# Crossed quadrants for two of four pairs in an inversion by halves, in a twelve-stage decoder kernel on one core

## The chip, the core and the metric

The kernel runs on one core of one Trainium2 chip. Its time is the device time of one execution in microseconds (us). The whole network, four layers of three stages each, runs in one launch; the four batch elements are four passes of a loop. The change touches the first stage of a pass only.

## The reference, cut to what matters

The first layer's attention is a gated delta rule over 512 tokens with 16 heads of 64 values, two heads of v for each head of q and k:

```python
def step(S, xs):
    q_t, k_t, v_t, g_t, b_t = xs
    S = S * jnp.exp(g_t)[..., None, None]
    kv = jnp.einsum('bhk,bhkv->bhv', k_t, S)
    S = S + jnp.einsum('bhk,bhv->bhkv', k_t, (v_t - kv) * b_t[..., None])
    o_t = jnp.einsum('bhk,bhkv->bhv', q_t, S)
    return (S, o_t)
S0 = jnp.zeros((b_, HV, DK, DV), jnp.float32)
_, oT = jax.lax.scan(step, S0, (qT, kT, vT, gT, bT))
```

Taken 128 tokens at a time this scan needs, for each head, the inverse of a unit lower triangular matrix of 128x128 that is made of k times k, the decays and b. The outputs, the state for the next 128 tokens, and all later stages follow from it.

## The kernel before, in words

The function `stage_l0_attn` computes the inverse by halves. The 128 rows are two blocks of 64, TOP (partitions 0 to 63) and LOW (64 to 127). In each block an inverse X of blocks of 1, 2, 4, ... rows is doubled level by level, L = 6 levels in all; levels 1 to 5 double inside the blocks, level 6 makes the corner between TOP and LOW. X and its transpose XT are both kept, in `xx` (index 0 and 1). A level l < 6 is: `half_level`, AX = part times X (L2622), where `part` is the level's share of the matrix, masked by GpSimd (L2810); a copy of AX from PSUM to `ax` by ScalarE (L2744); `whole_level`, the products X AX (L2637) and AX XT (L2641); and VectorE's subtraction of both from `xx` (L2912, at level 5 L2916 and L2919, which write `solved`). Level 6 is L2618, L2744 on 64 rows, L2632, and ScalarE's `corner` (L2752).

The heads are taken two at a time (a pair), four pairs in one step (p = 0 to 3), eight steps in a pass (n = 0 to 7; 128 tokens of half of the heads each). FIRST is the pairs 0 and 1, SECOND the pairs 2 and 3. PSUM bank p belongs to pair p of the inversion: columns 0 to 127 for AX, 128 to 255 for the change of X, 256 to 383 for that of XT. Every matmul on a block has 64 rows and 64 columns of TensorE, and for levels 1 to 5 it reads and writes the same block, TOP to TOP or LOW to LOW: two of the array's four quadrants. A f32 matmul is two MATMUL records in the trace.

Between the levels of step n every engine does, in an order written out by hand, the work around the inversion: of the coming step `prep` (L2532, L2536; decays by ScalarE L2694 and L2699; VectorE L2837 to L2843) and `turn` (L2544: the transpose of `part0`; VectorE L2854 and L2856 make the first XT and X from it), and of the past step `ks` (L2565, VectorE L2868), `corrected` (L2582, ScalarE L2724 and L2734), `output` (L2591, VectorE L2883 or a copy) and `add` (L2601, VectorE L2898). TensorE's order in a step:

- level 1: half, ks FIRST of the past, whole, prep FIRST of the coming
- level 2: half, corrected FIRST, whole
- level 3: half, output FIRST, whole, turn FIRST
- level 4: half, add FIRST, prep SECOND, whole, ks SECOND
- level 5: half, corrected SECOND, whole, output SECOND, turn SECOND
- level 6: half, whole, add SECOND

VectorE's order: ks FIRST, whole 1; whole 2, prep FIRST; output FIRST, whole 3, turn FIRST; add FIRST, whole 4, ks SECOND, prep SECOND; whole 5, turn SECOND; output SECOND, add SECOND. Step 0 has no past work, steps 1 and 2 no ks (their state products are still zero), step 7 no coming work.

Each engine goes through its queue in order, and waits on counting semaphores: `x_less` (VectorE's update of a pair is done), `ax_psum`, `ax_ready`, `xx_psum`, `part_ready`, `x0_ready` (the first X of a pair), `a_turned` (turn is done).

Of the kernel before, what the change touches and what calls it, by code (L numbers as in the profile page):

```python
# [21 lines left out]
ALU = mybir.AluOpType  # L22
# [3 lines left out]
P = 128  # L26
# [2182 lines left out]
def stage_l0_attn(m):  # L2209
# [16 lines left out]
    with ExitStack() as ctx:  # L2226
# [248 lines left out]
        a_turned = sem("a_turned")  # L2475
        x0_ready = sem("x0")
# [46 lines left out]
        with nc.Block(no_gpsimd_drain=True) as block:  # L2523
            @block.tensor
            def _(pe):
# [13 lines left out]
                def turn(n, pairs):  # L2539
                    for p in pairs:  # L2540
# [5 lines left out]
                        ins.then_inc(a_turned, 1)  # L2546

# [57 lines left out]
                def half_level(n, l):  # L2605

                    for p in range(4):
                        if l == 1:
                            pe.wait_ge(x0_ready, unit(n, p) + 1)
                            if n >= 1:  # L2610
                                pe.wait_ge(corner_ready, unit(n - 1, p) + 1)
                        else:
                            pe.wait_ge(x_less, at_less(n, l - 1, p))
                        if l < L:
                            pe.wait_ge(part_ready, at_less(n, l, p))
                        for i in range(2):
                            if l == L:
                                ins = pe.matmul(m.psum[LOW, p, W * i:W * i + W], ab[TOP, n % 2, p, i, W:P],  # L2618
                                                xx[TOP, n % 2, p, X, i, :], start=True, stop=True)
                            else:  # L2620
                                for b in BLOCKS:
                                    ins = pe.matmul(m.psum[b, p, W * i:W * i + W], part[b, (M * n + l - 1) % 2, p, i, :],  # L2622
                                                    xx[b, n % 2, p, X, i, :], start=True, stop=True)
                        ins.then_inc(ax_psum, 1)

                def whole_level(n, l):

                    for p in range(4):
                        pe.wait_ge(ax_ready, at(n, l, p))
                        if l == L:  # L2630
                            for i in range(2):
                                ins = pe.matmul(m.psum[TOP, p, 256 + W * i:256 + W * i + W], ax[LOW, p, i, :],  # L2632
                                                solved[LOW, n % 2, p, i, W:P], start=True, stop=True)
                        else:
                            for i in range(2):
                                for b in BLOCKS:
                                    pe.matmul(m.psum[b, p, P + W * i:P + W * i + W], xx[b, n % 2, p, XT, i, :],  # L2637
                                              ax[b, p, i, :], start=True, stop=True)
                            for i in range(2):
                                for b in BLOCKS:  # L2640
                                    ins = pe.matmul(m.psum[b, p, 256 + W * i:256 + W * i + W], ax[b, p, i, :],  # L2641
                                                    xx[b, n % 2, p, XT, i, :], start=True, stop=True)
                        ins.then_inc(xx_psum, 1)
# [9 lines left out]
                for pairs in (FIRST, SECOND):  # L2653
                    prep(0, pairs)
                    turn(0, pairs)
                for n in range(STEPS + 1):
# [769 lines left out]
```

## Time and profile before

| | |
|---|---|
| median of 3 runs | 4809.8 us (4809.14 to 4811.06) |
| profiled execution | 4809.4 us |
| its span, first to last instruction | 4807.6 us |
| granted TensorE clock, mean | 0.922 |
| TensorE matmul / weight load busy | 4044.5 us (84%) / 2481.0 us (52%) |
| VectorE / ScalarE / GpSimd busy | 2463.6 (51%) / 1545.1 (32%) / 820.3 us (17%) |

The profiled execution is 1.8 us longer than its span. A busy share of TensorE is of modelled ends: matmuls are pipelined, each record of a 64x64 f32 matmul lasts 0.22 us, and many are in flight at a time, so that starts say more than durations. In pass 1 the eight steps of the inversion begin at 120.6 us; in pass 2 they begin at 1322.7 us.

### The profile page before, as it was taken

Reading aid. Unit: us, or ns where it says so; the run is one execution under the profiler, and the core shown is the slowest. Engines: PE = TensorE matmul, PEld = TensorE weight load, DVE = VectorE, ACT = ScalarE, POOL = GpSimd, SP = SyncE. Lnnn points to the kernel's source line nnn. Section 1 sums busy time; section 2 is a strip of 40 time slices with the busy share of each in tenths; the row PEclk is TensorE's granted clock in tenths of the full one; section 3 lists DMA queues with packets and bytes.
Section 4 is the critical chain, followed back from the end, with each engine's and each line's share of the span. In section 5 each row is a group of like instructions: output and inputs, shape, how many; then the busy total and the mean of one; then the engine's idle time right before and its main releaser. Section 6 shows DMA issues by size and latency. Waiting matters only on the chain. (4 is left out here: it accounts for less than half of the span.)

```text
span 4807.6 us, 96693 instructions
## 1 busy us (share of the span) xinstructions
PE 4044.5 (84%) x38412; PEld 2481.0 (52%) x38412; DVE 2463.6 (51%) x6030; ACT 1545.1 (32%) x3476; POOL 820.3 (17%) x1436
## 2 busy tenths in 40 slices
PE   6997787898799778789879977878987998787888
PEld 3884343465388334346548833434654873343464
DVE  5664444454566443445456645345545664533554
ACT  3442222341344222234134422223413442222341
POOL 1430000130143000013014300001201430001120
PEclk8999999999799999999979999999997999999999
DMA  2000000000000000000000010000000001000000
GB/s 79 3 3 16 41 18 17 22 35 25 25 3 3 16 41 18 17 22 35 25 25 3 3 39 18 18 17 22 35 25 25 3 3 56 1 18 17 22 35 27
DMA packets 11006, 105.56 MB, mean 22 GB/s; under 512 B 1149, under 2 KB 5553, under 8 KB 6193
## 3 DMA queue, kind: packets, MB, share of 16 engines
q1 hardware_dynamic: 10544, 99.21, 5.4%
q8 instruction: 314, 5.14, 0.4%
q14 instruction: 148, 1.20, 0.1%
HBM read 98.16 MB, written 1.05 MB: 21 GB/s over the span
## 5 line engine op out<-in xcount | busy, mean ns | idle before, releaser
L88 PE MATMUL psum<-ident_bf 128*128 128x512 bf16 x1928 | 540.6, 420 | 201.5 <-DVE l_attn_peak L770 66.5
L88 PEld LDWEIGHTS psum<-ident_bf 128*128 128x128 bf16 x1928 | 190.7, 106 | 480.1 <-issue 170.6
L2912 DVE TENSOR_TENSOR l_attn_xx<-l_attn_xx,psum 128x256 f32<-128x256 f32 x512 | 206.1, 419 | 209.6 <-PE psum L2641 197.4
L2744 ACT ACTIVATE l_attn_ax<-psum 128x128 f32<-128x128 f32 (+1 forms) x768 | 184.7, 279 | 357.0 <-PE psum L2622 242.3
L399 DVE TENSOR_TENSOR l_ffn_hidden<-l_ffn_silu,psum 128x512 f32<-128x512 f32 (+2 forms) x184 | 126.4, 687 | 325.2 <-ACT l_ffn_silu L340 325.1
L94 PEld LDWEIGHTS psum<-streamed_weights,l_ffn_hidden 128*128 128x128 f32 (+2 forms) x1728 | 226.0, 192 | 113.4 <-issue 100.2
L340 ACT ACTIVATE l_ffn_silu<-psum 128x512 f32<-128x512 f32 (+2 forms) x216 | 128.9, 597 | 475.9 <-PE psum L310 475.9
L2637 PE MATMUL psum<-l_attn_ax,l_attn_xx 64*64 64x64 f32 x5120 | 266.0, 222 | 0.0
L2641 PE MATMUL psum<-l_attn_xx,l_attn_ax 64*64 64x64 f32 x5120 | 259.2, 220 | 0.0
L770 DVE TENSOR_REDUCE l_attn_peak<-psum 128x4 f32<-128x2048 f32 (+3 forms) x128 | 185.8, 1487 | 122.7 <-PE psum L688 121.7
L2810 POOL TENSOR_TENSOR l_attn_part<-l_attn_ab,streamed_weights 128x128 f32<-128x128 f32 x640 | 242.6, 414 | 27.4 <-PE psum L2622 27.4
L94 PE MATMUL psum<-streamed_weights,l_ffn_hidden 128*128 128x128 f32 (+2 forms) x1728 | 229.9, 276 | 9.1 <-DVE l_ffn_hidden L396 5.0
L787 DVE RECIPROCAL l_attn_inverse<-psum 128x512 f32<-128x512 f32 x20 | 67.2, 3358 | 292.5 <-PE psum L722 292.5
L2637 PEld LDWEIGHTS psum<-l_attn_ax,l_attn_xx 64*64 64x64 f32 x5120 | 205.9, 136 | 17.3 <-issue 9.3
L746 ACT ACTIVATE l_attn_prob<-psum 128x2048 f32<-128x2048 f32 (+1 forms) x96 | 152.9, 1593 | 184.7 <-PE psum L707 184.7
L2641 PEld LDWEIGHTS psum<-l_attn_xx,l_attn_ax 64*64 64x64 f32 x5120 | 206.2, 137 | 0.0
L2622 PE MATMUL psum<-l_attn_xx,l_attn_part 64*64 64x64 f32 x5120 | 197.7, 224 | 8.4 <-POOL l_attn_part L2810 6.0
L2622 PEld LDWEIGHTS psum<-l_attn_xx,l_attn_part 64*64 64x64 f32 x5120 | 177.6, 137 | 28.1 <-issue 13.4
L164 ACT ACTIVATE xnT<-psum 128x256 f32<-128x256 f32 x80 | 29.9, 384 | 463.1 <-PE psum L177 459.2
L309 PE MATMUL psum<-l_ffn_gated_x,streamed_weights 128*128 128x512 f32 (+1 forms) x320 | 169.4, 611 | 4.5 <-DVE l_ffn_gated_x L378 4.5
L760 POOL TENSOR_SCALAR_AFFINE_SELECT l_attn_prob<-l_attn_prob 128x512 f32<-128x512 f32 x128 | 80.0, 637 | 540.6 <-ACT l_attn_prob L746 540.6
L2431 DVE SCALAR_TENSOR_TENSOR l_attn_conv<-psum,streamed_weights,l_attn_conv 128x511 f32<-128x511 f32 (+2 forms) x192 | 142.3, 748 | 54.8 <-ACT l_attn_conv L2361 50.3
(514 smaller groups left out, 8131.1 us busy)
## 6 DMA issues: line engine op xcount, KB each, us to landing
streamed_weights<-pack_l_ffn SPq DMA_DIRECT2D x4, 5412.0 KB, 16.5
streamed_weights<-pack_l_ffn SPq DMA_DIRECT2D x4, 3972.0 KB, 12.6
streamed_weights<-pack_l_attn SPq DMA_DIRECT2D x5, 2848.5 KB, 9.5
streamed_weights<-pack_l_xattn SPq DMA_DIRECT2D x4, 2496.0 KB, 8.6
streamed_weights<-pack_l_ffn SPq DMA_DIRECT2D x4, 2192.0 KB, 8.3
streamed_weights<-pack_l_xattn SPq DMA_DIRECT2D x4, 2048.0 KB, 8.5
streamed_weights<-pack_l_ffn SPq DMA_DIRECT2D x4, 1923.0 KB, 8.1
streamed_weights<-pack_l_attn SPq DMA_DIRECT2D x4, 1107.5 KB, 5.2
```

The lines of the kernel that those rows point to most:

```text
L88: pe.matmul(self.bank(bank), self.ident_bf[:, :], self.ident_bf[:, :].unsqueeze(1).to_broadcast([P, NT, P]), start=True, stop=True)
L94: ins = pe.matmul(self.psum[:, OUT, t * P:(t + 1) * P], features[:, t * P:(t + 1) * P], weight, start=first and t == 0, stop=last, skip_gr ...
L309: pe.matmul(m.bank(n % 2)[0:r], w["up"][:, c:c + r], rhs, start=True, stop=True)
L746: act.activation(prob[:, u % SLOTS, :, 0:used(part)], m.psum[:, 0:R, 0:used(part)], ACT.Exp).then_inc(exps_ready, 1)
L770: dve.tensor_reduce(peak[:, g, i, :], m.psum[:, base:base + R, 0:(i + 1) * P], AX, ALU.max, negate=True).then_inc(peak_ready, 1)
L2431: ins = dve.scalar_tensor_tensor(out=later, in0=m.psum[:, n % 2, 0:T - 3 + i], scalar=w["conv_w"][:, ORDER[n], i:i + 1], in1=later, op0=AL ...
L2622: ins = pe.matmul(m.psum[b, p, W * i:W * i + W], part[b, (M * n + l - 1) % 2, p, i, :], xx[b, n % 2, p, X, i, :], start=True, stop=True)
L2637: pe.matmul(m.psum[b, p, P + W * i:P + W * i + W], xx[b, n % 2, p, XT, i, :], ax[b, p, i, :], start=True, stop=True)
L2641: ins = pe.matmul(m.psum[b, p, 256 + W * i:256 + W * i + W], ax[b, p, i, :], xx[b, n % 2, p, XT, i, :], start=True, stop=True)
L2744: act.activation(ax[b, p, :, :], m.psum[b, p, 0:P].rearrange("p (i t) -> p i t", i=2), ACT.Copy).then_inc(ax_ready, 1)
L2810: pool.tensor_tensor(part[:, q % 2, p, :, :], ab[:, n % 2, p, :, 0:W], over_block(w["levels"][:, l, :]), ALU.mult).then_inc(part_ready, 1)
L2912: dve.tensor_tensor(both, both, m.psum[:, p, P:384], ALU.subtract).then_inc(x_less, 1)
```

## The change

For the odd pairs (p = 1 and 3, "crossed") the half level's product reads block b and writes the other block, and the X product of the whole level comes back the same way. So the plain pair uses the quadrants TOP to TOP and LOW to LOW, and the crossed pair TOP to LOW and LOW to TOP. In `xx` the crossed pair has X and XT in swapped places (`kind`), with XT on the other block than X. ScalarE gives `ax` a scale of -1 for crossed pairs, and VectorE adds where it subtracted. The XT product of a crossed pair, for levels 1 to 4, reads and writes one block, into columns 384 to 511 of the plain neighbour's bank; at level 5 it goes across, on top of an identity product that carries the old XT across.

The products of two pairs are now issued interleaved, after the waits of both. VectorE's update of a plain pair waits for its neighbour's products too. To bring the first XT of a crossed pair onto the other block there is a new step `move` of TensorE (one identity product per head and block, into the place in PSUM that `turn` filled, hence after VectorE has taken X from there, `x0_taken`), and of VectorE (the subtraction from the identity). TensorE has it after half level 4 (FIRST) and half level 6 (SECOND), VectorE at the start of its levels 4 and 6.

```diff
+        def crossed(p):
+            return p % 2 == 1
+        def side(p, b):
+            return {0: LOW, W: TOP}[b.start] if crossed(p) else b
+        def kind(p, which):
+            return 1 - which if crossed(p) else which
...
+                def move(n, pairs):
+                    for p in pairs:
+                        if crossed(p):
+                            pe.wait_ge(a_turned, unit(n, p) + 1)
+                            pe.wait_ge(x0_taken, unit(n, p) // 2 + 1)
+                            for i in range(2):
+                                for b in BLOCKS:
+                                    ins = pe.matmul(m.psum[side(p, b), 4 + p % 2, W * i:W * i + W],
+                                                    w["ident_blocks"][b, :], part0[b, p % 2, i, :], start=True, stop=True)
+                            ins.then_inc(moved, 1)
...
                 def half_level(n, l):
-                    for p in range(4):
...
+                    def product(p, i, b):
+                        return pe.matmul(m.psum[side(p, b), p, W * i:W * i + W], part[b, (M * n + l - 1) % 2, p, i, :],
+                                         xx[b, n % 2, p, kind(p, X), i, :], start=True, stop=True)
+
+                    for pairs in (FIRST, SECOND):
...
                         if l < L:
+                            for i in range(2):
+                                for p in pairs:
+                                    for b in BLOCKS:
+                                        ins = product(p, i, b)
+                                    if i == 1:
+                                        ins.then_inc(ax_psum, 1)
...
                 def whole_level(n, l):
+                    def x_product(p, i, b):
+                        s = side(p, b)
+                        pe.matmul(m.psum[b, p, P + W * i:P + W * i + W], xx[s, n % 2, p, kind(p, XT), i, :], ax[s, p, i, :],
+                                  start=True, stop=True)
+
+                    def xt_product(p, i, b):
+                        s = side(p, b)
+                        old = xx[s, n % 2, p, kind(p, XT), i, :]
+                        if crossed(p) and l == M:
+                            out = m.psum[b, p, 256 + W * i:256 + W * i + W]
+                            pe.matmul(out, w["ident_blocks"][s, :], old, start=True, stop=False)
+                            return pe.matmul(out, ax[s, p, i, :], old, start=False, stop=True)
+                        out = m.psum[s, p - 1, 384 + W * i:384 + W * i + W] if crossed(p) else \
+                            m.psum[s, p, 256 + W * i:256 + W * i + W]
+                        return pe.matmul(out, ax[s, p, i, :], old, start=True, stop=True)
+
+                    for pairs in (FIRST, SECOND):
+                        for p in pairs:
+                            pe.wait_ge(ax_ready, at(n, l, p))
...
                         if n < STEPS:
                             half_level(n, l)
+                        if l == 4:
+                            coming(n, move, FIRST)
+                        elif l == 6:
+                            coming(n, move, SECOND)
...
+                        act.activation(ax[b, p, :, :], m.psum[b, p, 0:P].rearrange("p (i t) -> p i t", i=2), ACT.Copy,
+                                       scale=-1.0 if crossed(p) and l < L else 1.0).then_inc(ax_ready, 1)
...
-                        dve.tensor_tensor(xx[:, n % 2, p, XT, :, :], one, part0[:, p % 2, :, :], ALU.subtract)
+                        if not crossed(p):
+                            dve.tensor_tensor(xx[:, n % 2, p, XT, :, :], one, part0[:, p % 2, :, :], ALU.subtract)
...
+                def move(n, pairs):
+                    one = w["ident_blocks"].unsqueeze(1).to_broadcast([P, 2, W])
+                    for p in pairs:
+                        if crossed(p):
+                            dve.wait_ge(moved, unit(n, p) // 2 + 1)
+                            dve.tensor_tensor(xx[:, n % 2, p, kind(p, XT), :, :], one, heads(m.psum[:, 4 + p % 2, 0:P]),
+                                              ALU.subtract).then_inc(x0_ready, 1)
...
-                        dve.wait_ge(xx_psum, at(n, l, p))
+                        dve.wait_ge(xx_psum, at(n, l, p if crossed(p) else p + 1))
```

## Rows read from the trace of the kernel before

**Rows 1.** The page: engines busy; costliest groups (busy, mean ns, idle before, releaser).

```profile
PE 4044.5 (84%) x38412; PEld 2481.0 (52%) x38412; DVE 2463.6 (51%) x6030; ACT 1545.1 (32%) x3476; POOL 820.3 (17%) x1436
...
L2637 PE MATMUL psum<-l_attn_ax,l_attn_xx 64*64 64x64 f32 x5120 | 266.0, 222 | 0.0
```

**Rows 2.** Windows, whole steps: us, then busy us of each engine, granted clock, DMA.

```profile
147.45:176.62 29.17, 28.73 (x607) 25.96 (x605) 18.27 (x59) 14.05 (x55) 12.81 (x28) 0.92 0.01 3
1349.03:1376.23 27.20, 26.76 (x602) 23.91 (x600) 18.36 (x59) 13.82 (x55) 12.80 (x28) 1.00 0.01 3
233.08:262.06 28.98, 28.28 (x617) 25.07 (x617) 20.98 (x73) 14.85 (x60) 12.82 (x28) 1.00 0.01 3
1322.65:1349.03 26.38, 24.05 (x561) 21.39 (x561) 16.82 (x52) 10.49 (x39) 15.25 (x35) 0.93 0.01 3
```

**Rows 3.** Order of time, TensorE in a steady step: start, us, engine, line, count.

```profile
236.81 1.13 PE L2532 MATMUL psum<-l_attn_gu,w_const 128*128 128x256 f32 x4
237.88 0.70 PE L2536 MATMUL psum<-l_attn_qk 64*128 64x256 f32 x4
...
240.90 0.40 PE L2641 MATMUL psum<-l_attn_xx,l_attn_ax 64*64 64x64 f32 x8
...
242.30 0.40 PE L2641 MATMUL psum<-l_attn_xx,l_attn_ax 64*64 64x64 f32 x8
...
248.44 0.44 PE L2601 MATMUL psum<-l_attn_u_end,l_attn_k 128*64 128x128 f32 x4
...
250.50 0.45 PE L2637 MATMUL psum<-l_attn_ax,l_attn_xx 64*64 64x64 f32 x8
```

**Rows 4.** Order of time, VectorE in the same step, levels 2 and 3.

```profile
241.35 1.82 DVE L2912 TENSOR_TENSOR l_attn_xx<-l_attn_xx,psum 128x256 f32<-128x256 f32 x4 [4.00 <-PE psum L2641]
243.09 0.41 DVE L2837 TENSOR_TENSOR l_attn_ab<-l_attn_decay,psum 64x256 f32<-64x256 f32 x1
...
246.39 1.41 DVE L2912 TENSOR_TENSOR l_attn_xx<-l_attn_xx,psum 128x256 f32<-128x256 f32 x4
```

**Rows 5.** Order of time, TensorE where level 6's half meets turn.

```profile
258.79 0.27 PE L2618 MATMUL psum<-l_attn_xx,l_attn_ab 64*64 64x64 f32 x1
258.83 0.28 PE L2544 MATMUL psum<-streamed_weights,l_attn_part 64*64 64x64 f32 x3
258.89 0.22 PE L2618 MATMUL psum<-l_attn_xx,l_attn_ab 64*64 64x64 f32 x1
258.90 0.27 PE L2544 MATMUL psum<-streamed_weights,l_attn_part 64*64 64x64 f32 x2
...
259.01 0.70 PE L2618 MATMUL psum<-l_attn_xx,l_attn_ab 64*64 64x64 f32 x9
```

**Rows 6.** Order of time, all engines, the steady step's end.

```profile
256.81 0.28 DVE L2916 TENSOR_TENSOR l_attn_xx<-l_attn_xx,psum 128x128 f32<-128x128 f32 x1
...
260.06 0.42 DVE L2854 TENSOR_TENSOR l_attn_xx<-streamed_weights,l_attn_part 128x128 f32<-128x128 f32 x1
260.08 0.27 PE L2618 MATMUL psum<-l_attn_xx,l_attn_ab 64*64 64x64 f32 x1 [0.37 <-DVE l_attn_solved L2919]
...
260.32 1.01 PE L2632 MATMUL psum<-l_attn_solved,l_attn_ax 64*64 64x64 f32 x13
...
260.86 0.78 ACT L2752 ACTIVATE l_attn_solved<-psum 64x128 f32<-64x128 f32 x4
...
261.53 0.60 PE L2601 MATMUL psum<-l_attn_u_end,l_attn_k 128*64 128x128 f32 x4 [0.20 <-DVE l_attn_v L2883]
```

**Rows 7.** Windows, columns as in rows 2: pass 1, pass 2, a steady step's end.

```profile
145.20:151.90 6.70, 6.53 (x108) 6.34 (x110) 2.72 (x9) 2.51 (x10) 1.12 (x4) 0.50 0.00 0
...
142.50:145.00 2.50, 1.53 (x24) 0.98 (x18) 2.36 (x11) 0.36 (x2) 2.37 (x6) 1.00 0.03 7
1345.00:1348.00 3.00, 1.64 (x23) 1.09 (x20) 2.82 (x12) 0.82 (x3) 3.00 (x9) 1.00 0.02 5
257.50:260.90 3.40, 3.03 (x55) 2.80 (x53) 3.22 (x13) 1.06 (x5) 2.84 (x8) 1.00 0.00 0
```

More of the change, by code:

```diff
@@ L2475, in stage_l0_attn @@
         a_turned = sem("a_turned")
+        x0_taken = sem("x0_taken")
+        moved = sem("moved")
         x0_ready = sem("x0")
@@ L2605, in half_level @@
                 def half_level(n, l):
-                    for p in range(4):
[L2608 to L2613, printed above, removed]
-                        if l < L:
-                            pe.wait_ge(part_ready, at_less(n, l, p))
-                        for i in range(2):
-                            if l == L:
[L2618 to L2630, printed above, removed]
-                            for i in range(2):
[L2632 to L2643, printed above, removed]
+                    def product(p, i, b):
+                        return pe.matmul(m.psum[side(p, b), p, W * i:W * i + W], part[b, (M * n + l - 1) % 2, p, i, :],
+                                         xx[b, n % 2, p, kind(p, X), i, :], start=True, stop=True)
@@ new lines, in whole_level @@
+                def whole_level(n, l):
+                    def x_product(p, i, b):
[15 more added lines that the diff above has]
+                            pe.wait_ge(ax_ready, at(n, l, p))
+                            if l == L:
+                                for i in range(2):
+                                    ins = pe.matmul(m.psum[TOP, p, 256 + W * i:256 + W * i + W], ax[LOW, p, i, :],
+                                                    solved[LOW, n % 2, p, i, W:P], start=True, stop=True)
+                                ins.then_inc(xx_psum, 1)
+                        if l < L:
+                            for i in range(2):
+                                for p in pairs:
+                                    for b in BLOCKS:
+                                        x_product(p, i, b)
+                            for p in pairs:
+                                for i in range(2):
+                                    for b in BLOCKS:
+                                        ins = xt_product(p, i, b)
+                                ins.then_inc(xx_psum, 1)
@@ L2655, in _ @@
                     turn(0, pairs)
+                    move(0, pairs)
                 for n in range(STEPS + 1):
@@ L2910, in whole_level @@
                         if l < M:
-                            both = xx[:, n % 2, p, :, :, :].rearrange("p a i t -> p (a i t)")
-                            dve.tensor_tensor(both, both, m.psum[:, p, P:384], ALU.subtract).then_inc(x_less, 1)
+                            both = xx[:, n % 2, p, :, :, :].rearrange("p a i t -> p a (i t)")
+                            if crossed(p):
+                                change = m.psum[:, p - 1:p + 1, :].rearrange("p n c -> p (n c)")[:, 384:896].rearrange(
+                                    "p (a c) -> p a c", a=2)[:, :, 0:P]
+                                ins = dve.tensor_tensor(both, both, change, ALU.add)
+                            else:
+                                change = m.psum[:, p, P:384].rearrange("p (a c) -> p a c", a=2)
+                                ins = dve.tensor_tensor(both, both, change, ALU.subtract)
+                            ins.then_inc(x_less, 1)
                         else:
@@ L2925, in _ @@
                     turn(0, pairs)
+                    move(0, pairs)
                 for n in range(STEPS + 1):
@@ L2933, in _ @@
                             output(n - 1, FIRST)
+                        if more and l == 4:
+                            move(n + 1, FIRST)
+                        if more and l == 6:
+                            move(n + 1, SECOND)
                         if last and l == 4:
```

33 lines of the change are left out of this document (25 added, 8 removed).

## The prediction

> **What bounds the kernel now.** I read the page first, for the engines' shares and the lines of the first layer's inversion [rows 1]; then the stage's steps one by one, which say what a step costs and at which clock [rows 2]; then the order of time inside one steady step, TensorE and VectorE side by side, since only that shows which wait ends last [rows 3 to 6]; and last the granted clock around the one place where it fell inside the stage [rows 7].
>
> The stage is four passes (one per batch element) of eight steps. A steady step takes 28.98 us, of which TensorE is busy 28.28 and VectorE 20.98 at a granted clock of 1.00 [rows 2]. So the naive reading is that TensorE bounds it, and that fewer TensorE microseconds are worth their full price. The order of time says less. Level 3's x updates run on VectorE back to back, four in 1.41 us (0.33 us from start to start), behind a preparation that began at 243.09; level 2's four came at TensorE's pace, 1.82 us [rows 4]. At the end of the step TensorE waits outright: L2618 of the last pair starts at 260.08, right after VectorE's L2919, and L2601 at 261.53 after L2883 [rows 6]. VectorE has 20.7 us of starts per step and each group of them hangs on a TensorE result. I count time inside the steady step from 233.08 = 0.
>
> **Beats.** A 64x64 f32 matmul is two records. Groups of eight records on the two diagonal quadrants follow each other every 0.23 us (240.90 to 242.30 is six of them [rows 3]), so two records, one per quadrant, start each 58 ns: I call this a beat. Do other quadrants run beside them? The trace of before has the case: L2618 goes from the upper rows to the lower columns. Its records start at 258.79, 258.89 and 259.01 with one between the last two, and among them L2544, on the diagonal, keeps starting at 258.83 and 258.90 [rows 5]. So three quadrants run at a beat each, although two of them share their rows and two their columns. I take four records per beat for the changed kernel.
>
> The Trainium skill, "TensorE: Matmul & The Clock Gate", Part 3 (What overlaps and what doesn't), says that a weight load overlaps a running matmul only where their row groups differ, which speaks against this change: a plain and a crossed pair share row groups. By the rule TensorE would save nothing; the row above is against it, and the last rival is what it would give.
>
> **Part by part, TensorE per step.**
> - Half levels 1 to 5: 16 beats each become 8 (two groups of 4): 40 beats less, 2.34 us.
> - Whole levels 1 to 4: per two pairs 8 + 8 beats become 4 beats of x products on four quadrants, then 8 of XT products, which stay on the diagonal in both pairs: 8 less per level, 32 in all, 1.87 us.
> - Whole level 5: the crossed pairs' XT products go across and have an identity product added. Plain quadrants carry 4+4 beats, crossed ones 4+8, so 12 per two pairs if they overlap (16, as now, if not): 0.47 us or nothing. It is hidden either way, since VectorE is the later one there.
> - Added: two moves a step, 4 beats each, 0.23 us and a first beat of 0.05.
>
> Sum: 28.28 - 4.7 + 0.6, about 24.2 us of TensorE in a step. VectorE keeps the same number of instructions: a crossed pair's L2854 goes, the move's subtraction comes; L2919's subtraction becomes a copy. ACT's scale of -1 costs nothing: L2752 copies with it, four in 0.78 us [rows 6], as fast as any plain copy of ACT.
>
> **What waits are added.** Each pair of pairs is now waited for together, in half_level, whole_level and in VectorE's plain pair. The move is a round trip: VectorE's x0 of the crossed pair, TensorE's move, VectorE again. Behind TensorE's wait for it at level 4 stand add and prep of SECOND and whole level 4; at level 6 whole level 6 and add of SECOND. Latencies: from a last record's start to its reader 0.27 us (the group that starts at 242.30 and lasts 0.40 has its last start at 242.48 [rows 3], and the fourth update starts 0.42 before the end of its row, at 242.75 [rows 4]); from an instruction's end to a waiting TensorE 0.05 (VectorE's level 5 ends at 260.03, L2618 starts at 260.08 [rows 6]).
>
> **The steady step, chained by hand.** Level 1: half 0 to 0.5, ks to 1.3, whole to 2.75, prep (L2532 and L2536, 236.81 to 238.51, 1.7 us [rows 3]) to 4.6; before 5.43. Level 2: half to 5.1, corrected to 6.25, whole to 7.65. VectorE's prep starts when level 2's updates are through, at 8.65 for 10.0 before: 1.36 us are gained here. Level 3: VectorE runs without a gap, prep 2.78, output 0.53, four updates 1.33 [rows 4], and the crossed x0 ends 0.75 later (by the turn of SECOND, which starts at 260.06 [rows 6]), at 14.03. TensorE's move waits for it, so add starts at 14.4 for 15.36, and whole level 4 at 16.5 for 17.42 [rows 3]: of 1.36 us 0.9 are left. Whole level 4 is 0.47 shorter, so VectorE's prep of SECOND starts at 19.6 for 20.96: 1.36 again. From there VectorE is the bound: prep 2.78, four times 0.81 for level 5 (256.81 to 260.06 [rows 6]), ending at 25.65. The x0 of SECOND is done at 26.55; TensorE's move runs 26.6 to 26.85; whole level 6 (L2632, 16 records on one quadrant, one per beat, as x13 in 1.01 us) ends its starts at 27.8; add and the switch of shapes 0.7 as at 261.53 to 262.06, next step at 28.5. Before whole level 6 started at 27.02 beside the last L2618; now it starts at 26.9 for all of VectorE's lead. So a steady step gains 0.5 us of the 4.1 that TensorE saves.
>
> **The others.** Steps 1 and 2 have no state products: 27.20 us at full clock [rows 2]. The same chain gains 0.9 at level 2's end, 0.5 at add, 0.6 at VectorE's second prep, and the end gives 0.85 back: 0.2 us slower. Step 0: level 1 is cold (clock 0.93 over the step), the shorter products gain 0.9, given back at the end: 0. Step 7 has no next step to prepare, so no moves: 1.0 faster (bounds 0.5 and 1.3). Before step 0 the move lies open once: 0.9 slower. Steps 3 to 6: 4 x 0.5. Per pass 2.0 - 0.4 + 0 + 1.0 - 0.9 = 1.7 us faster, four passes 6.8. Each hand-made step may be off by 0.5 us either way, one way in all: 32 x 0.5 = 16 us.
>
> **The clock.** That sum holds at 2.4 GHz. In pass 1 the clock fell to 1.2 GHz (0.50) at the end of step 0 and stayed there for the 6.70 us of the row [rows 7]. What TensorE did before: short bursts of L2618 between waits for VectorE, busy 1.53 of 2.50 us. In pass 2 the same place was busy 1.64 of 3.00 and the clock held; so too in passes 3 and 4. In the steady step the place is dense, 3.03 of 3.40, and it never fell. The price: step 1 took 29.17 us in pass 1 and 27.20 in pass 2 [rows 2], 1.97 us. After the change every step's end looks like step 0's: TensorE has done output and turn at 24.1 and until 26.9 it has three bursts of L2618 and the move, about 1.6 us of record time in 3.0. It then faces level 1 and 2, where TensorE is the path and VectorE idle, so a low clock is paid in full. There are 7 such ends in a pass, 28 in all. One in four fell in the rows; by the single-quadrant stretch that follows (move, then whole level 6) I take two in five: 11, which is 10 more than before, 19.7 us. Ends: none (clock holds) and half of them plus the tails, 18, 34 us.
>
> Sum against the profiled execution, 4809.4 us (span 4807.6, 1.8 around it; the median is 4809.8): 4809.4 - 6.8 + 19.7 = 4822.3 us.
>
> **Rivals.**
> - The clock holds. For it: three of four sparse ends of step 0 held. Against: 28 chances. 4809.4 - 6.8 = 4802.6 us.
> - TensorE is the bound as its share says. For it: 28.28 of 28.98. All of it reaching the end gives 4.1 x 32 = 131 us, 4678; VectorE's gapless stretch [rows 4] is against. Its milder form, 1.0 us a step more than my chain, because waits overlap better than I drew, gives 4802.6 - 28 = 4775, or with five falls 4785.
> - Quadrants that share rows take turns. TensorE then saves nothing, the moves lie open: 0.4 us at level 4 and 0.9 at the step's end, 28 x 1.3 = 36 us: 4846 us. [rows 5] is against it; the skill's rule of Part 3 named above would give this.
>
> **How the numbers follow.** A measurement of this kernel can tell 0.2%, 9.6 us, from no change, so the bounds are 4800.2 and 4819.4. The forecast, falls of the clock at the steps' ends: 0.47, of it 0.42 above the bound and 0.05 (few falls) inside. Clock holds: 0.28, of it 0.05 below. More gained than my chain has: 0.20, all faster. Turns: 0.05, slower. So faster 0.25, same 0.28, slower 0.47. The likeliest case alone spans 4811 (seven falls, less gain) to 4843 (18 falls, chain gain near 0). The range must take in the clock-holds case with some of its error, down to 4795, and leaves the rest of the third case and the last outside: 4795 to 4843.
>
> **What would show it.** Right: L2622's 32 records in about half their time when both groups are ready; steady steps of about 28.5 us where the clock is 1.00; gaps in TensorE at the end of levels 2, 3 and 5, released by VectorE; TensorE's move waiting for the crossed x0 with whole level 6 behind it; granted clock 0.50 at some steps' starts, two in five, mean clock about 0.915 for 0.922. Wrong: a clock of 1.00 through all steady steps (then 4803), steady steps under 28 us (the hand chain has a wait too many), or L2637's crossed records 58 ns behind the plain ones (turns).

## The result, and the profile after

The changed kernel takes 4878.3 us (median of 4 runs, 4872.6 to 4884.9) beside 4810.4 us for the kernel before on the same chip (4 runs): ratio 1.014, 95% interval 1.0122 to 1.0157. The forecast was 4822.3 us with a range to 4843. The sign was right, the size was not. The profiled execution took 4881.4 us (span 4879.7), which is 72.0 us more than that of before; I forecast 12.9 more. TensorE's busy time hardly moved, by the first lines of the page (busy us and share of the span):

```profile
PE 4037.4 (83%) x39436; PEld 2431.4 (50%) x39436; DVE 2445.9 (50%) x6030; ACT 1535.0 (31%) x3476; POOL 817.0 (17%) x1436
...
L2633 PE MATMUL psum<-l_attn_xx,l_attn_part 64*64 64x64 f32 x5120 | 151.2, 244 | 56.0 <-DVE l_attn_xx L2982 33.0
L2663 PE MATMUL psum<-l_attn_ax,l_attn_xx 64*64 64x64 f32 x5120 | 172.8, 241 | 2.3 <-ACT l_attn_ax L2800 2.3
```

L2663 was L2637, with 266.0 us [rows 1]; the half level's product is now L2633. The second line's end is the new thing: TensorE waits 56.0 us ahead of the half levels, most of it for VectorE's update of a crossed pair (L2982).

Windows of whole steps after, columns as in [rows 2]: step 0, two second steps (pass 1 and 2), a third step, two steady steps, and all of pass 1's inversion:

```profile
121.40:150.56 29.16, 23.95 (x593) 19.75 (x593) 16.32 (x52) 10.04 (x39) 14.79 (x34) 0.85 0.01 3
150.56:180.10 29.54, 26.52 (x635) 22.59 (x633) 17.70 (x58) 13.64 (x54) 12.74 (x28) 0.90 0.01 3
1363.70:1393.20 29.50, 26.49 (x636) 22.59 (x635) 17.64 (x58) 13.67 (x54) 12.74 (x28) 0.90 0.01 3
180.12:209.77 29.65, 26.57 (x634) 22.54 (x632) 18.27 (x60) 13.07 (x52) 12.74 (x28) 0.90 0.01 3
239.78:270.93 31.15, 28.22 (x648) 23.98 (x648) 20.57 (x72) 14.68 (x60) 12.73 (x28) 0.89 0.02 4
270.93:300.66 29.73, 26.84 (x650) 22.72 (x648) 20.58 (x72) 14.57 (x60) 12.73 (x28) 0.95 0.01 3
121.40:348.24 226.84, 201.84 (x4894) 171.23 (x4896) 143.03 (x485) 100.47 (x407) 94.64 (x212) 0.91 0.01 3
```

Before, a steady step took 28.98 us at 1.00 and a second step 27.20 [rows 2]. Now none of these windows has a clock of 1.00. The last column but two is to be read first: 0.85 to 0.95. Windows around the ends of steps, as in [rows 7], and one of the few ends at which the clock held:

```profile
178.50:185.30 6.80, 6.60 (x114) 5.70 (x113) 2.49 (x9) 1.91 (x8) 0.00 (x0) 0.50 0.01 2
239.90:243.30 3.40, 3.40 (x76) 3.06 (x77) 1.68 (x8) 1.62 (x8) 0.00 (x0) 0.50 0.02 7
267.20:274.00 6.80, 6.28 (x94) 5.33 (x94) 3.00 (x14) 2.54 (x12) 0.00 (x0) 0.50 0.01 2
297.00:300.40 3.40, 2.30 (x34) 1.99 (x36) 2.43 (x10) 1.52 (x7) 1.19 (x4) 1.00 0.00 0
```

In pass 1 TensorE went down to 1.2 GHz at the ends of six of the seven steps that have a next one; all passes together, at 24 of 28, and twice more in the middle of step 0 (passes 2 and 4), where before it was 1 of 28. Summed over the four inversions the trace has 171.9 us of low clock, for 21.4 before (some 15 of these are left over from the stretch ahead of the inversions); the inversions themselves take 911.8 us, for 855.2 (from the start of a pass's first half-level record to the start of its last one, at level 5 of step 7). So 56.6 of the 72.0 us lie inside them.

What the end of a steady step looks like, TensorE, at full clock (start, us, engine, line; in brackets the idle time before and who ended it), and VectorE beside it. This is the end of step 5, at which the clock held:

```profile
297.14 0.44 PE L2648 MATMUL psum<-l_attn_xx,l_attn_ab 64*64 64x64 f32 x4 [0.18 <-DVE l_attn_solved L2996]
297.96 0.44 PE L2648 MATMUL psum<-l_attn_xx,l_attn_ab 64*64 64x64 f32 x4 [0.38 <-DVE l_attn_solved L2994]
298.98 0.45 PE L2569 MATMUL psum<-l_attn_part,streamed_weights 64*64 64x64 f32 x8 [0.58 <-DVE l_attn_xx L2915]
299.27 1.09 PE L2682 MATMUL psum<-l_attn_solved,l_attn_ax 64*64 64x64 f32 x16
300.30 0.44 PE L2626 MATMUL psum<-l_attn_u_end,l_attn_k 128*64 128x128 f32 x4
300.66 0.86 PE L2633 MATMUL psum<-l_attn_xx,l_attn_part 64*64 64x64 f32 x32
```

```profile
297.94 0.40 DVE L2913 TENSOR_TENSOR l_attn_xx<-streamed_weights,l_attn_part 128x128 f32<-128x128 f32 x1
298.35 0.48 DVE L2915 TENSOR_TENSOR l_attn_xx<-streamed_weights,psum 128x128 f32<-128x128 f32 x2
299.47 0.29 DVE L2923 TENSOR_TENSOR l_attn_xx<-streamed_weights,psum 128x128 f32<-128x128 f32 x1 [0.63 <-PE psum L2569]
```

The move (L2569) cannot start until VectorE has made the last x0 (L2915), and level 6's whole (L2682, L2632 of before) stands behind it. Before, L2632 had its first record at 260.10 beside the last L2618, 0.04 us after VectorE came to its last turn at 260.06 [rows 6]; now it starts 1.33 us after VectorE's last turn (297.94 to 299.27):

```profile
260.10 0.27 PE L2632 MATMUL psum<-l_attn_solved,l_attn_ax 64*64 64x64 f32 x1
```

The end of step 3 looked the same, and there the clock fell at 239.9; the end of step 6, where it fell at 328.6, too:

```profile
236.14 0.44 PE L2648 MATMUL psum<-l_attn_xx,l_attn_ab 64*64 64x64 f32 x4 [0.18 <-DVE l_attn_solved L2996]
236.96 0.44 PE L2648 MATMUL psum<-l_attn_xx,l_attn_ab 64*64 64x64 f32 x4 [0.38 <-DVE l_attn_solved L2994]
237.98 0.45 PE L2569 MATMUL psum<-l_attn_part,streamed_weights 64*64 64x64 f32 x8 [0.58 <-DVE l_attn_xx L2915]
...
326.95 0.44 PE L2648 MATMUL psum<-l_attn_xx,l_attn_ab 64*64 64x64 f32 x4 [0.38 <-DVE l_attn_solved L2994]
```

So the same idle times stand at ends that fell and at one that held. What decides between them no run here shows.

### The profile page after: what moved, and what is told of

Its sections match the earlier page's. It is cut to its first block and busy times, and to the rows that moved or that the text cites. A ratio compares the mean times of both kernels' runs of the same rounds, so it can differ in the third digit from the quotient of the medians.

```text
span 4879.7 us, 99197 instructions
## 1 busy us (share of the span) xinstructions
PE 4037.4 (83%) x39436; PEld 2431.4 (50%) x39436; DVE 2445.9 (50%) x6030; ACT 1535.0 (31%) x3476; POOL 817.0 (17%) x1436
## 5 line engine op out<-in xcount | busy, mean ns | idle before, releaser
L2800 ACT ACTIVATE l_attn_ax<-psum 128x128 f32<-128x128 f32 (+1 forms) x768 | 167.8, 278 | 386.4 <-PE psum L2633 281.8
L2985 DVE TENSOR_TENSOR l_attn_xx<-l_attn_xx,psum 128x256 f32<-128x256 f32 x256 | 107.3, 419 | 227.0 <-PE psum L2675 226.8
L2675 PE MATMUL psum<-l_attn_xx,l_attn_ax 64*64 64x64 f32 x4608 | 207.0, 231 | 0.1
L2633 PE MATMUL psum<-l_attn_xx,l_attn_part 64*64 64x64 f32 x5120 | 151.2, 244 | 56.0 <-DVE l_attn_xx L2982 33.0
L2675 PEld LDWEIGHTS psum<-l_attn_xx,l_attn_ax 64*64 64x64 f32 x4608 | 180.0, 147 | 0.4 <-issue 0.4
L2663 PE MATMUL psum<-l_attn_ax,l_attn_xx 64*64 64x64 f32 x5120 | 172.8, 241 | 2.3 <-ACT l_attn_ax L2800 2.3
L309 PE MATMUL psum<-l_ffn_gated_x,streamed_weights 128*128 128x512 f32 (+1 forms) x320 | 169.4, 611 | 4.5 <-DVE l_ffn_gated_x L378 4.5
L2633 PEld LDWEIGHTS psum<-l_attn_xx,l_attn_part 64*64 64x64 f32 x5120 | 117.7, 148 | 96.4 <-DVE l_attn_xx L2982 67.4
L310 PE MATMUL psum<-l_ffn_gated_x,streamed_weights 128*128 128x512 f32 (+1 forms) x320 | 163.4, 592 | 0.0
```

The lines of the kernel that those rows point to most:

```text
L309: pe.matmul(m.bank(n % 2)[0:r], w["up"][:, c:c + r], rhs, start=True, stop=True)
L310: pe.matmul(m.bank(2 + n % 2)[0:r], w["gate"][:, c:c + r], rhs, start=True, stop=True).then_inc(up_ready, 1)
L2633: return pe.matmul(m.psum[side(p, b), p, W * i:W * i + W], part[b, (M * n + l - 1) % 2, p, i, :], xx[b, n % 2, p, kind(p, X), i, :], start ...
L2663: pe.matmul(m.psum[b, p, P + W * i:P + W * i + W], xx[s, n % 2, p, kind(p, XT), i, :], ax[s, p, i, :], start=True, stop=True)
L2675: return pe.matmul(out, ax[s, p, i, :], old, start=True, stop=True)
L2800: act.activation(ax[b, p, :, :], m.psum[b, p, 0:P].rearrange("p (i t) -> p i t", i=2), ACT.Copy, scale=-1.0 if crossed(p) and l < L else 1 ...
```

## The experiments

The theories. A: what costs is the clock, which falls because TensorE's work at a step's end has become sparse. B: what costs is the added waits themselves, the pairs waited for together and the round trip of the move, at full clock. The further question was which piece of the change makes the end sparse.

Each was timed against the kernel before on the same chip; between the chips the kernel before differs by up to 3 us, so the ratios compare the kernels best. Low clock and inversion time in the table are sums over the four inversions of the profiled execution.

| kernel | us | ratio to before | steady step, us | inversions, us | low clock in them, us |
|---|---|---|---|---|---|
| before | 4810 | 1 | 28.98 | 855.2 | 21.4 |
| changed | 4878.3 | 1.014 (1.0122 to 1.0157) | 29.5 to 31.9 | 911.8 | 171.9 |
| e1: changed, filled ends | 4830.3 | 1.005 (1.0033 to 1.0068) | 29.06 | 872.3 | 37.7 |
| e2: before, filled ends | 4826.8 | 1.0037 (1.0025 to 1.005) | 29.46 | 864.3 | 13.8 |
| e3: pairs only, no crossing | 4852.5 | 1.0082 (1.0064 to 1.0101) | 29.72 | 896.6 | 26.4 |
| e4: both moves late | 4807.9 | 0.9991 (0.9979 to 1.0003) | 27.94 | 841.2 | 52.2 |
| e5: before with one wait | 4863.6 | 1.0109 (1.0093 to 1.0124) | 30.7 to 32.1 | 917.4 | 124.1 |
| e6: second move late | 4813.8 | 0.9996 (0.9985 to 1.0007) | 27.97 | 847.2 | 64.2 |
| e7: both late, step 0 filled | 4794.8 | 0.9967 (0.9955 to 0.9978) | 27.90 | 831.9 | 21.1 |
| e8: before, step 0 filled | 4805.4 | 0.9991 (0.9982 to 1.0001) | 29.01 | 853.3 | 14.0 |

**e1, the changed kernel with its ends filled.** Products that nobody reads stand ahead of TensorE's waits at the step's end.

```diff
+                def fill(count, bank):
+                    for _ in range(count):
+                        pe.matmul(m.psum[TOP, bank, 384:512], m.ident_bf[:, 0:W], m.ident_bf[:, :], start=True, stop=True)
...
+                                if l == L and p >= 1:
+                                    fill(4, p - 1)
                                 pe.wait_ge(x_less, at_less(n, l - 1, p))
...
                         elif l == 6:
+                            if n + 1 < STEPS:
+                                fill(4, 3)
                             coming(n, move, SECOND)
```

> The changed kernel with four small bf16 products (128 rows, 64 columns, 128 moving) before each wait for VectorE at level 6 and before the second move, where TensorE waits about 0.5 us each time. Theory A (the clock: it falls at the end of 24 of 28 steps, and that is the whole loss, since steps with little low clock take the 29.0 us of before): the clock stays at 1.00 through most steps, low time inside the stage falls from 165 us to under 60, steps of 29.0 to 29.3 us, 4815 to 4830 us. Theory B (the added waits are the loss and the clock is a bystander): the steps stay at 29.5 to 31.5 us plus the fill, 4878 or more.

**e2, the same fill in the kernel before**, ahead of level 6's waits, to price it.

```diff
+                            if l == L and p >= 1:
+                                fill(4, p - 1)
                             pe.wait_ge(x_less, at_less(n, l - 1, p))
```

> Control: the kernel before with the same products before the waits of level 6. Both theories: the stage was at full clock there already but for pass 1, so nothing to win beyond 2 us; the change of shapes costs at most 3 x 0.15 us a step where TensorE did not wait. 4808 to 4825 us.

A steady step and the whole inversion of pass 1, first of e1, then of e2:

```profile
234.52:263.58 29.06, 27.28 (x666) 22.95 (x664) 20.62 (x72) 14.69 (x61) 12.78 (x28) 1.00 0.02 4
121.80:338.05 216.25, 198.37 (x5005) 166.96 (x5008) 143.01 (x485) 100.25 (x407) 94.88 (x212) 0.99 0.01 4
```

```profile
232.05:261.51 29.46, 29.33 (x632) 25.85 (x630) 21.05 (x72) 14.92 (x60) 12.82 (x28) 1.00 0.01 3
120.60:336.70 216.10, 214.19 (x4756) 190.33 (x4756) 147.64 (x486) 103.73 (x408) 95.47 (x213) 0.99 0.01 3
```

More work on TensorE made the changed kernel 48 us faster. The low clock went from 171.9 to 37.7 us, and the step to 29.06 us at a clock of 1.00. The fill isn't free: three groups a step (the changed kernel has a fourth, ahead of the move) cost the kernel before 0.48 us a step (29.46 against 28.98) and 17 us in all, which is 2 us above the expected 4825. In the changed kernel a part of the fill stands in time in which TensorE would wait, so less than that is to be taken off; its own rows give 28.9 to 29.0 us for a steady step at full clock (see "The parts, added up"). Theory A's numbers hold, at their upper end, so most of the loss is the clock.

**e3, waits without crossing.** All pairs are plain and there are no moves; the order of the products and the waits for two pairs stay.

```diff
         def crossed(p):
-            return p % 2 == 1
+            return False
...
-                        dve.wait_ge(xx_psum, at(n, l, p if crossed(p) else p + 1))
+                        dve.wait_ge(xx_psum, at(n, l, p | 1))
```

> The changed kernel's loops and pair waits with no pair crossed, so no move and only the two diagonal quadrants. Theory A: TensorE has the beats of before (28.3 us in 29), is dense at the step's end, the clock holds, 4810 to 4825 us. Theory B, in the form that waiting for two pairs at a time costs: VectorE's first update is 0.47 us later at each of five levels, steps of 30 us or more at full clock, 4835 to 4880 us.

```profile
240.09:269.81 29.72, 28.51 (x619) 25.05 (x618) 20.74 (x73) 14.62 (x60) 12.80 (x28) 1.00 0.01 3
123.70:348.03 224.33, 212.81 (x4672) 187.65 (x4672) 144.21 (x486) 100.61 (x408) 95.21 (x212) 0.99 0.01 3
```

The waits in pairs have a price of their own, 0.74 us in a steady step and 2.3 in step 7 (18.48 us for 16.19, to its last half level), 41 us over the four inversions, but the clock stays up (26.4 us low): it falls at the end of step 0, in all four passes, and at no later end. So they don't bring the falls of the other steps. The time is what theory B expected, the clock what theory A did. This kernel also shows what crossing does to the products. A half level's 32 records at full clock, first here, then in the changed kernel:

```profile
245.50 1.15 PE L2633 MATMUL psum<-l_attn_xx,l_attn_part 64*64 64x64 f32 x32
```

```profile
276.82 0.70 PE L2633 MATMUL psum<-l_attn_xx,l_attn_part 64*64 64x64 f32 x32
```

Each row is 0.22 us longer than its starts: 0.93 and 0.48 us for 16 and 8 beats.

**e4, both moves late.** TensorE's move FIRST goes behind add FIRST, its move SECOND behind the whole of level 6; VectorE's move SECOND goes behind output SECOND.

```diff
-                        if l == 4:
-                            coming(n, move, FIRST)
-                        elif l == 6:
-                            coming(n, move, SECOND)
...
                             past(n, add, FIRST)
+                            coming(n, move, FIRST)
                             coming(n, prep, SECOND)
...
+                            coming(n, move, SECOND)
                             past(n, add, SECOND)
...
-                        if more and l == 6:
-                            move(n + 1, SECOND)
...
                             output(n - 1, SECOND)
+                        if more and l == 6:
+                            move(n + 1, SECOND)
```

> The changed kernel with the second move behind whole level 6 instead of ahead of it (VectorE's part behind its output), and the first behind add. The hand chain says whole level 6 starts 0.8 us earlier and the step is 0.7 to 0.9 us shorter in 28 steps, clock falls unchanged: 4853 to 4860 us. Rival: the next step's half level 1 then waits for the x0 of the last pair and gets all of it back: 4870 to 4880 us. If the denser end also keeps the clock up in some steps: under 4850 us.

The end of a steady step, and windows of such a step and of the inversion:

```profile
283.72 0.44 PE L2648 MATMUL psum<-l_attn_xx,l_attn_ab 64*64 64x64 f32 x4 [0.18 <-DVE l_attn_solved L2994]
284.54 0.27 PE L2648 MATMUL psum<-l_attn_xx,l_attn_ab 64*64 64x64 f32 x1 [0.38 <-DVE l_attn_solved L2992]
...
284.78 1.01 PE L2682 MATMUL psum<-l_attn_solved,l_attn_ax 64*64 64x64 f32 x13
285.57 0.45 PE L2569 MATMUL psum<-l_attn_part,streamed_weights 64*64 64x64 f32 x8
285.95 0.44 PE L2626 MATMUL psum<-l_attn_u_end,l_attn_k 128*64 128x128 f32 x4
286.32 0.88 PE L2633 MATMUL psum<-l_attn_xx,l_attn_part 64*64 64x64 f32 x32
```

```profile
230.34:258.28 27.94, 25.71 (x651) 21.58 (x648) 20.50 (x73) 14.42 (x60) 12.74 (x28) 1.00 0.01 4
121.10:330.38 209.28, 188.47 (x4893) 158.88 (x4896) 142.31 (x485) 98.72 (x407) 94.65 (x212) 0.98 0.01 4
```

The gaps of 0.18 and 0.38 us are still there; the one of 0.58 is gone. From the start of the last L2648 group to the next step it is now 1.78 us (284.54 to 286.32), for 2.70 in the changed kernel (297.96 to 300.66), both at full clock. The time is below the figures that both theories gave by the chain; what came true is the clause on a denser end. The same products, the moves among them put elsewhere, take 70 us less, and the clock no longer falls in any steady step. What low clock is left lies in step 0, where it also falls in the middle in two passes, and in the first 4 us of step 1.

**e5, the kernel before with that one wait.** TensorE waits for the last x0 ahead of level 6's whole; nothing else is changed.

```diff
+                        if l == L and n + 1 < STEPS:
+                            pe.wait_ge(x0_ready, unit(n + 1, 3) + 1)
                         if n < STEPS:
                             whole_level(n, l)
```

> The kernel before with one wait more: TensorE's whole level 6 waits until VectorE has made the last pair's x0 of the coming step, as the move of SECOND makes it wait in the changed kernel. No crossing, no move. The wait holds whole level 6 back by VectorE's last turn, about 0.75 us (L2854 of SECOND starts at 260.06 in the steady step, the first record of L2632 at 260.32, a crossed x0 ends at about 260.8 to 261). Theory A (a wait for VectorE at the step's end costs itself, and the sparse end then lets TensorE's clock fall): steady steps 29.5 to 29.9 us at full clock, the clock falls at many of the 28 step ends, low clock in the stage 60 us or more against 21, in all 4840 to 4870. Theory B (the wait costs only itself; the falls come from the shorter products of the crossed kernel): steady steps 29.5 to 29.9, low clock in the stage 20 to 35 us, in all 4825 to 4838. If the wait is hidden by the last L2618 (a third way): steps 29.0 to 29.2, 4810 to 4816.

```profile
262.94 0.44 PE L2618 MATMUL psum<-l_attn_xx,l_attn_ab 64*64 64x64 f32 x4 [0.37 <-DVE l_attn_solved L2921]
264.09 1.14 PE L2632 MATMUL psum<-l_attn_solved,l_attn_ax 64*64 64x64 f32 x16 [0.71 <-DVE l_attn_xx L2858]
265.17 0.44 PE L2601 MATMUL psum<-l_attn_u_end,l_attn_k 128*64 128x128 f32 x4
265.53 1.27 PE L2622 MATMUL psum<-l_attn_xx,l_attn_part 64*64 64x64 f32 x19
```

```profile
265.60:269.00 3.40, 3.40 (x49) 3.06 (x50) 1.31 (x6) 1.11 (x4) 0.00 (x0) 0.50 0.02 5
234.17:265.59 31.42, 30.21 (x620) 26.79 (x619) 21.16 (x72) 15.23 (x60) 12.78 (x28) 0.93 0.01 3
118.10:346.94 228.84, 219.46 (x4672) 195.88 (x4672) 147.78 (x486) 105.45 (x408) 95.39 (x213) 0.93 0.01 3
```

One idle time of 0.71 us, in the kernel before, brings 51 us and 124 us of low clock; the clock falls at 21 of 28 ends. Crossed quadrants are not needed for the loss. Theory A's numbers hold (124.1 us low for "60 or more", 4863.6 for "4840 to 4870"). The wait holds whole level 6 back by more than the 0.75 us named there, since in the kernel before its first record stands at 260.10 and not at 260.32.

**e6, only the second move late**: e4's edit without its move of FIRST, which stays ahead of add FIRST.

> The changed kernel with only the second move (SECOND, at the step's end) taken away from its place: TensorE's half of it behind the whole of level 6, VectorE's behind output SECOND. The first move stays ahead of add FIRST. With both moves late the kernel took 4807.85 us, steady steps 27.9 us at full clock, low clock in the stage 52 us. Theory A (the whole excess of the changed kernel comes from the second move): steady steps 27.9 to 28.1, low clock 40 to 65 us, 4806 to 4814. Theory B (the first move's round trip at level 4 holds add and whole level 4 back by 0.5 us or more): steady steps 28.4 or more, 4820 to 4830.

```profile
235.00:262.97 27.97, 25.65 (x654) 21.65 (x652) 20.60 (x72) 14.43 (x60) 12.76 (x28) 1.00 0.01 4
```

27.97 against 27.94: the first move costs next to nothing where it stood. The second is the whole excess over this kernel. Theory A's numbers hold.

**e7, a candidate for the best version.** e4 and, in step 0 alone, products that nobody reads.

```diff
+                        if n == 0 and l == 4 and pairs == FIRST:
+                            fill(8)
                         for p in pairs:
+                            if n == 0 and l == L and p >= 1:
+                                fill(5)
```

> Both moves late, and in step 0 of each pass bf16 products of 128x128 that nobody reads: eight before level 4's half of FIRST, five before each wait of level 6. What low clock is left with both moves late lies at the end of step 0 and in step 1 (1284.6 to 1346.1 and 148.0 to 151.4, 52 us over four passes, about 0.35 us of time per us of it). Theory A (these falls come from the sparse end of step 0): the low clock in the stage falls to 25 us or less, 4796 to 4804. Theory B (they come from what stands before the stage or from phase, and the added products cost their own time): low clock 40 us or more, 4808 to 4816.

Step 0, a steady step, and pass 1's inversion:

```profile
124.50:151.86 27.36, 24.07 (x615) 19.65 (x616) 16.03 (x51) 10.11 (x40) 14.81 (x34) 0.89 0.01 3
232.92:260.82 27.90, 25.67 (x650) 21.54 (x648) 20.51 (x73) 14.44 (x60) 12.75 (x28) 1.00 0.02 4
124.50:332.63 208.13, 189.34 (x4916) 159.22 (x4919) 142.35 (x485) 98.77 (x407) 94.67 (x212) 0.99 0.01 4
```

**e8, the kernel before with e7's fill.**

> The kernel before with the same products that nobody reads in step 0 of each pass (eight before level 4's half, five before each wait of level 6 from the second pair on), no crossing. It says how much of e7's 17 us under the kernel before is the clock of step 0 and how much the crossed quadrants. The kernel before has 21 us of low clock in the stage, of which one fall at the end of step 0 in pass 1 costs 1.97 us; at 0.35 us of time per us of low clock all of it is worth 7 us. Theory A (the crossing itself brings the gain of e7): 4803 to 4812, stage 848 to 856 us. Theory B (the gain of e7 is the fill's): 4795 to 4800, stage 840 us or less.

```profile
233.67:262.68 29.01, 28.31 (x617) 25.10 (x616) 20.98 (x73) 14.83 (x60) 12.80 (x28) 1.00 0.01 3
```

e7 is under both kernels: 0.33% under before, and 83 us under the changed one, which was timed on another chip. The fill alone gives the kernel before 0.09%, with an interval that touches 1. So some two thirds of e7's gain comes with the crossing, once its move stands where it holds nothing up. Both times are close to what was expected for theory A: 4794.8 us is 1 us under its range, and 4805.4 lies in it.

**The parts, added up.** What is a microsecond of low clock worth in time? Step 1 of e6 took 28.21 us with 4.0 us low and its step 2 26.54 with none: 0.42. The kernel before gives 0.44 (step 1 of pass 1 and 2, [rows 2], 4.5 us low), the changed kernel's two steady steps above 0.36 (31.15 with 7.1 low, 29.73 with 3.1). No one rate fits all kernels, so here is every inversion time at full clock by two of them:

| | inversions at full clock, us, at 0.42 | difference | at 0.36 | difference |
|---|---|---|---|---|
| before | 846.2 | | 847.5 | |
| with pair waits (e3) | 885.5 | +39.3 | 887.1 | +39.6 |
| and crossed, moves late (e4) | 819.3 | -66.2 | 822.4 | -64.7 |
| and the first move in its place (e6) | 820.2 | +0.9 | 824.1 | +1.7 |
| and the second (the changed kernel) | 839.6 | +19.4 | 849.9 | +25.8 |
| before with the wait alone (e5) | 865.3 | +19.1 on before | 872.7 | +25.2 on before |

Only the price of the wait at the step's end hangs on the rate, and it can be read without one, between records that all ran at full clock. In the changed kernel the last L2648 group and the next step start 2.70 us apart, in e4 1.78: the wait costs 0.92 us, 25.8 for 28 ends. In e5 the last L2618 group and the next step start 2.59 us apart (262.94 to 265.53), in the kernel before 1.98 (260.08 [rows 6] to 262.06): 0.61 us, 17 for 28 ends. What stands ahead of the last group takes nearly the same with either place of the move: 26.29 us in step 6 of the changed kernel (300.66 to 326.95; 26.19 in the other passes), 26.13 in step 6 of e4, all at full clock. So the changed kernel's steady step at full clock takes 28.9 to 29.0 us, hardly less than the 28.98 of before. The start of the next step, in the kernel before:

```profile
262.06 0.27 PE L2622 MATMUL psum<-l_attn_xx,l_attn_part 64*64 64x64 f32 x2
```

This speaks for 0.36 in the changed kernel, as a mean: against 28.9 to 29.0 us, its steady steps in pass 1 pay about 0.25 to 0.45 for a microsecond of low clock, by where in the step it lies. With 0.36 the inversions at full clock are 2.4 us longer than before, and the clock takes 0.36 x 150.5 = 54 of the 56.6 us. With 0.42 it would take 63, and the change would gain 6.6 us at full clock. Either way the loss is nearly all clock, and what crossing gives is used up by the waits. The Trainium skill, "TensorE: Matmul & The Clock Gate", Terms, puts the penalty at low time times one minus the clock's share, half a microsecond per microsecond; an estimate by it is 75 us. The steps here show 0.36 to 0.44, less where TensorE has more idle time; that this is the reason was not tested.

## Why the prediction was wrong in size

By its steps:

- **Beats: right.** Four records to a beat, 32 in 0.70 us. L2663 and L2675 of two pairs run on all quadrants. Quadrants that share rows do not take turns, which refutes the rival. The rule of the Trainium skill, "TensorE: Matmul & The Clock Gate", Part 3 (What overlaps and what doesn't), that a weight load overlaps a running matmul only in another row group, does not hold for these products.
- **TensorE's busy time per step: too low.** 25.7 us in a steady step at full clock (e4) for 28.28, where I had about 24.2: 2.6 us saved, not 4.1. It bears on nothing else, since the path was chained by starts.
- **Level 3: right.** VectorE runs without a gap there, and the first move costs nothing measurable.
- **The hand-chained steady step, 28.5: 0.4 to 0.5 too short.** At full clock it is 28.9 to 29.0 (above), which is within the 0.5 us allowed for each step, but is the whole gain. The end is as chained (2.70 us from the last L2648 group, 2.8 in the chain). What is missing is VectorE's lead: it comes to its last turn 26.3 us into the step (300.66 to 326.92), where the chain had 25.65 and before it was 27.0.
- **The other steps.** Steps 1 and 2: 27.2 to 27.5 at full clock by the two rates, forecast 0.2 more than before, 27.4: right. Step 0: 0.6 to 0.9 us slower by the same rates, for 0. Step 7: it has no move, and e4's stayed at full clock, 16.19 us to its last half level as before (314.23 to 330.42), 16.08 at the least. So it gains 0.1 at most, for 1.0 with a lower bound of 0.5. In the inversions all this makes 2.4 us slower (at 0.36), for 10.4 faster by the terms without the prologue (6.8 + 4 x 0.9).
- **The prologue: hardly there.** From the start of the last turn to that of the first half level it takes 2.51 us for 2.20 in pass 1: 0.3 for 0.9. The first half level had waited for GpSimd's part before too. Its start alone (121.4 us for 120.6) says nothing, since it scatters from 118.1 to 124.5 us over the runs.
- **The clock: this step failed.** The prediction said "I take two in five: 11, which is 10 more than before, 19.7 us". It was 24 of 28, 23 more, and some 2.4 us each for 1.97 (the 54 us above; 2.7 at 0.42). The number of falls makes 13 x 1.97 = 26 us of the miss, the price of one 23 x 0.4 = 9. The place was right (steps' ends), and so was the mechanism. But I took the frequency from step 0 of the kernel before, where three ends of four held, and added a little for the single-quadrant stretch. I did not set the new end beside it: I had worked out 1.6 us of record time in 3.0, about that of the end that did fall (1.53 of 2.50 [rows 7]), and gave 18 falls as the end of the range. Four passes over one end are also hardly four samples: falls mostly repeat from pass to pass (in the changed kernel the same six ends in all four, in e6 the end of step 0 in all four).
- **Outside the inversions: left out.** The rest of the kernel is 15.5 us longer, of which I had 3.6 (four prologues). The prologues are 1.3 of it. What follows step 7 until the past's last output is longer by 0.8 us a pass, 3 us. All kernels with pair waits have 3956 to 3968 us outside the inversions, the others 3946 to 3953, and they also have more low clock there, 720 to 751 us for 705 to 733. A line through the ten traces has 0.35 us of time for each of low clock; for the changed kernel, with 744.0 against 732.8, that is 4 us (an estimate, in part the same time as the 3 us). What is left is open, and so is why the clock falls more there.

The miss of 59.1 us is thus clock 34.5, inversions 12.8, rest 11.9 (at 0.42: 43.5, 3.8 and 11.9). In the sum over cases too much went to few falls, 0.28 for none.

Of the rivals, "TensorE is the bound" failed for the changed kernel, but its milder form is nearly e4: 27.9 us a step, a microsecond less than before, had the move been placed behind whole level 6. I had costed the move only where it stood, and found there the loss of all of VectorE's lead; I didn't follow what that wait does to the density of the end.

## What to carry to other kernels

A wait that opens a gap in TensorE's work is charged twice: once for itself (0.92 us here, 0.61 in e5) and again for the clock (some 2.4 us at each fall), when it joins other short gaps just before a stretch in which TensorE is the path. Put a round trip to another engine behind the work that does not need it, not ahead; here that alone is worth 70 us. Where a change also moves the clock, look for stretches that stayed at full clock on both sides and compare those; an average price of low clock can turn a small loss into a gain. To estimate falls, set the new stretch beside those of the trace that fell and that held, and let the range reach to a fall at every one.

## What was not expected of the hardware

- The mean share of TensorE's busy time does not tell its clock. In pass 1's inversion the changed kernel is busy 201.84 of 226.84 us (89%) at 0.91, e4 188.47 of 209.28 (90%) at 0.98, and e5 219.46 of 228.84 (96%) at 0.93. What the first and the last have and e4 has not is one idle time of 0.6 to 0.7 us at the end of each step.
- The ends that fell have no long idle time: 0.18, 0.38 and 0.58 us in the rows of 236.14 to 237.98. With the first two alone (e4) the clock held at all 16 ends of steady steps. The Trainium skill, "TensorE: Matmul & The Clock Gate", Part 1 (A second HAM failure mode), tells of a kernel in which frequent short idle times between groups of matmuls make the clock swing. The trace agrees, and here it is 172 us of low clock for 21.
- All four quadrants work at once with f32 products of 64x64 and different weights: 32 records in 0.70 us, for 1.15 on two.
- The pairwise waits, which move no work, cost 39 us, more than half of what the crossing gives back.
